# Laying score minima, column terms and inverse sums out block by block, so that each is added in one wide pass

## The reference

```python
# layer 0: 8-head attention, log(clip(adj)) added to the logits, output projection, layer norm of x + out
logits = einsum('bhqd,bhkd->bhqk', q, k) / sqrt(DK) + log(clip(adj, 1e-8, None))[:, None]
out = einsum('bhqk,bhkd->bhqd', softmax(logits), v) @ Wo.T + bo
# layer 1: one head, logits q_i + k_j, masked, leaky, softmax, times feat_proj, + feats
# layer 2: 8-head attention with a bias a_i + c_j + log(adj + 1e-9) on the logits, + x
scores = scores + (a[:, :, None] + c[:, None, :] + b_g + log(adj + EPS))[:, None]
out = einsum('bhij,bjhd->bihd', softmax(scores), V) + x
# layer 3: as layer 1, with other weights
```

## Time and profile before

| What | Value |
|---|---|
| Runs | 1846.76 us median of 3 (1843.98 to 1847.98) |
| Profiled execution | 1851.17 us, span 1849.3 us |
| Mean granted TensorE clock | 0.984 of full |
| Matmuls in the trace | 28388, some 443 for each group |

### The profile page before, as it was taken

One profiled execution on the slowest core, in us unless ns is written; L12 is line 12 of the kernel. 1 busy time (PEld: TensorE's weight loads), 2 busy tenths in 40 slices (PEclk: granted clock), 3 DMA queues, 4 the chain that ended last, 5 costly groups with the idle time before them and its releaser, 6 DMA issues.

```text
span 1849.3 us, 68980 instructions
## 1 busy us (share of the span) xinstructions
PE 1777.7 (96%) x28388; PEld 1679.8 (91%) x28388; DVE 1597.8 (86%) x3486; ACT 1318.2 (71%) x3536; POOL 670.2 (36%) x731
## 2 busy tenths in 40 slices
PE   5899999999999999999999999999999999999985
PEld 5799999999999999999999999999999999999985
DVE  4589889889889889889889889889889889888884
ACT  3577777777777777777777777777777777777763
POOL 2234344344344244244334334334334334334321
PEclk7899999999999999999999999999999999999997
DMA  3010111111111111011011011011011011011000
GB/s 114 19 37 29 44 48 34 40 48 35 38 48 39 34 48 43 30 48 47 26 48 47 26 48 47 25 48 48 25 48 48 25 48 48 25 48 48 25 22 18
DMA packets 48260, 74.57 MB, mean 40 GB/s; under 512 B 5456, under 2 KB 21968, under 8 KB 47952
## 3 DMA queue, kind: packets, MB, share of 16 engines
q1 hardware_dynamic: 47376, 69.49, 11.9%
q10 hardware_dynamic: 576, 0.68, 0.1%
HBM read 53.37 MB, written 16.78 MB: 38 GB/s over the span
## 4 chain that ended last, share of the span: by engine, by line
PE 71%; DVE 21%; issue 6%; ACT 1%; DMA 0%; POOL 0%; DVEq 0%; SPq 0%; POOLq 0%; ACTq 0%
PE banks L870 12%; PE banks L923 12%; PE banks L871 9%; PE banks L872 9%; PE banks L967 7%; PE banks L1062 6%; PE banks L958 6%; DVE xt_lo L650 6%; DVE weights_B L779 5%; DVE logits L723 3%; PE banks L973 3%; DVE logits L719 2%; PE banks L1056 2%; PE banks L1050 2%; PE banks L1022 2%
## 5 line engine op out<-in xcount | busy, mean ns | idle before, releaser
L431 POOL TENSOR_TENSOR xb_t<-sum_t,cols_tile 128x512 f32<-128x512 f32 x128 | 133.2, 1041 | 307.8 <-DVE sum_t L741 301.2
L478 POOL TENSOR_TENSOR weights_A<-weights_A,adj 128x512 f32<-128x512 f32 x64 | 82.5, 1289 | 407.4 <-ACT weights_A L548 407.4
L456 POOL TENSOR_TENSOR xt_lo<-x_t,xt_hi 128x512 fp32r<-128x512 f32 x64 | 82.4, 1288 | 317.1 <-ACT xt_hi L581 317.1
L630 ACT ACTIVATE logits<-logits,f_inv 128x128 f32<-128x128 f32 x256 | 89.0, 395 | 151.2 <-DVE f_inv L840 151.2
L755 DVE TENSOR_REDUCE least_cols_A<-banks 128x4 f32<-128x512 f32 x256 | 169.7, 685 | 15.3 <-PE banks L923 15.2
L779 DVE TENSOR_TENSOR weights_A<-banks,adj 128x512 f32<-128x512 f32 x192 | 132.4, 692 | 52.6 <-ACT banks L548 49.1
L870 PE MATMUL banks<-w_hi_v,xt_hi 128*128 128x258 f32 (+1 forms) x512 | 154.3, 301 | 13.0 <-DVE w_lo_v L650 9.8
L870 PE MATMUL banks<-w_hi_f,xt_hi 128*128 128x258 f32 x512 | 164.0, 320 | 0.8 <-DVE xt_lo L650 0.8
L755 DVE TENSOR_REDUCE least_B<-banks 128x4 f32<-128x512 f32 x256 | 163.9, 682 | 0.9 <-PE banks L932 0.9
L623 ACT ACTIVATE logits<-logits,f_neg_max 128x128 f32<-128x128 f32 x256 | 102.2, 411 | 85.7 <-DVE f_neg_max L726 85.7
L650 DVE TENSOR_TENSOR xt_lo<-sum_t,xt_hi 128x512 fp32r<-128x512 f32 x128 | 154.0, 1203 | 9.3 <-ACT xt_hi L581 2.1
(11 more groups left out here) (181 smaller groups left out, 6210.1 us busy)
## 6 DMA issues: line engine op xcount, KB each, us to landing
x_t<-x_t_dram SPq DMA_DIRECT2D x64, 256.0 KB, 3.6
x_in<-x_dram SPq DMA_DIRECT2D x64, 256.0 KB, 3.8
out_dram<-x_out SPq DMA_DIRECT2D x64, 256.0 KB, 2.4
adj_t<-adj_t_dram SPq DMA_DIRECT2D x64, 128.0 KB, 3.4
adj<-adj_dram SPq DMA_DIRECT2D x64, 128.0 KB, 2.0
scratch<-weights_dram SPq DMA_DIRECT2D x9, 256.0 KB, 7.0
...
```

The source lines that it names most:

```text
L431: return pool.tensor_tensor(result, x, col_tile.unsqueeze(2).broadcast_to([P, KT, GROUP * P]), ALU.add)
```

## The change

Three results that were written as one row for each unit now are written as four blocks of 128 columns, one for each unit, in which all rows but the unit's own are zero. A matmul with all rows of the row group and 512 columns then does for four units what a matmul for each did before.

- Minima and column term: VectorE in place of ScalarE reads the transposed bank, and multiplies it with a mask of 0 and 1 (`pick`) while it writes 128 x 512 elements. `shift` has 4 matmuls in place of 16, `column_terms` 4 in place of 8, all with 32 rows and 512 columns; `minus_pick` is gone, and the weights are `minus`, all -1.
- Inverse sums: VectorE writes both parts as before, now to `inv_both`; GpSimd multiplies them with a mask `own` to `inv_parts`, 128 x 512 (a new step `den` on GpSimd), and `wide` is one matmul of 512 columns with a `spread` of 128 x 128 that sums up the four former ones.
- `ORDER` is new on every engine, and so are some lags.

```diff
-        (0, "again", "A", 0), (0, "shift", "A", 0), (1, "fc", "1", 0), (1, "fc", "1", 1), (4, "turn_p", "3", 0),
...
+        (3, "again", "B", 0), (3, "shift", "B", 0), (4, "mask", "3", 0), (0, "k", "0", 0), (1, "out_proj", "0", 0),
...
+                    elif name == "den":
+                        if G.no == 0:
+                            pool.wait_ge(setup_dve, dve_step["own", "", ""])
+                        pool.wait_ge(inv_split[where], G.no + 1)
+                        pool.tensor_tensor(inv_parts[where][:, :, :],
+                                           inv_both[where][:, :].unsqueeze(1).broadcast_to([P, UNITS, P]),
+                                           own[:, :].unsqueeze(2).broadcast_to([P, UNITS, P]), ALU.mult
+                                           ).then_inc(inv_placed[where], 1)
...
-                    elif name == "turn_max":
-                        act.wait_ge(filled[b], turn.after(G, *key))
-                        act.activation(least_rows[where][:, :], bank[b][:, 0:P], ACT.Copy).then_inc(rows_ready[where], 1)
...
-                    elif name == "turn_rows":
-                        act.wait_ge(filled[b], turn.after(G, *key))
-                        act.activation(c_rows[:, :], bank[b][:, 0:P], ACT.Copy).then_inc(c_rows_ready, 1)
...
+                    elif name == "turn_max":
+                        dve.wait_ge(filled[b], turn.after(G, *key))
+                        dve.tensor_tensor(least_rows[where][:, :, :],
+                                          bank[b][:, 0:P].unsqueeze(1).broadcast_to([P, UNITS, P]),
+                                          pick[:, :].unsqueeze(2).broadcast_to([P, UNITS, P]), ALU.mult
+                                          ).then_inc(rows_ready[where], 1)
+                    elif name == "turn_rows":
+                        dve.wait_ge(filled[b], turn.after(G, *key))
+                        dve.tensor_tensor(c_rows[:, :, :, :],
+                                          bank[b][:, 0:P].unsqueeze(1).unsqueeze(1).broadcast_to([P, GROUP, 2, P]),
+                                          pick[:, 0:GROUP].unsqueeze(2).unsqueeze(2).broadcast_to([P, GROUP, 2, P]),
+                                          ALU.mult).then_inc(c_rows_ready, 1)
...
             def column_terms():
-                for g in range(GROUP):
-                    for r in range(HALF):
-                        part = row_group(r, GROUP)
-                        last = pe.matmul(bank[SCORE_BANKS[r]][:, cols(g, 2 * P)], minus_pick[part, g, :],
-                                         c_rows[part, :].unsqueeze(1).broadcast_to([GROUP, 2, P]),
-                                         start=False, stop=False, skip_group_check=True)
+                for r in range(HALF):
+                    part = row_group(r)
+                    last = pe.matmul(bank[SCORE_BANKS[r]], minus[part, :],
+                                     c_rows[part, :, :, :].rearrange("p g h m -> p (g h m)"),
+                                     start=False, stop=False, skip_group_check=True)
...
             def shift(s, G):
                 pe.wait_ge(rows_ready[s], G.no + 1)
-                for u in range(UNITS):
-                    for r in range(HALF):
-                        part = row_group(r, UNITS)
-                        last = pe.matmul(bank[SCORE_BANKS[r]][:, cols(u)], minus_pick[part, u, :],
-                                         least_rows[s][part, :], start=False, stop=True, skip_group_check=True)
+                for r in range(HALF):
+                    part = row_group(r)
+                    last = pe.matmul(bank[SCORE_BANKS[r]], minus[part, :],
+                                     least_rows[s][part, :, :].rearrange("p u n -> p (u n)"),
+                                     start=False, stop=True, skip_group_check=True)
...
             def wide(s, to):
-                for u in range(UNITS):
-                    last = pe.matmul(to[:, cols(u)], spread[:, u, :, :].rearrange("p r d -> p (r d)"),
-                                     inv_parts[s][:, :], start=True, stop=True)
-                return last
+                return pe.matmul(to[:, :], spread[:, :, :].rearrange("p r d -> p (r d)"),
+                                 inv_parts[s][:, :, :].rearrange("p u n -> p (u n)"), start=True, stop=True)
```

More of the change, by code:

```diff
@@ L27 @@
     "tensor": [
[7 rows of a table removed]
-    "vector": [
-        (3, "max_parts", "B", 0), (1, "split", "A", 0), (2, "mix", "1", 0), (4, "mask", "3", 0),
-        (1, "out_proj", "0", 0), (2, "turn_x", "2", 0), (3, "weigh", "B", 1), (3, "weigh", "B", 2),
-        (3, "weigh", "B", 3), (1, "out_proj", "0", 1), (0, "max", "A", 0), (4, "inv", "3", 0), (1, "norm", "", 0),
[5 rows of a table removed]
-    "scalar": [
[8 rows of a table removed]
[7 rows of a table added]
+    "vector": [
[4 rows of a table added]
+        (0, "out_proj", "0", 1), (3, "inv", "3", 0), (-1, "max", "A", 0), (-1, "max", "A", 1), (0, "norm", "", 0),
[4 rows of a table added]
+    "scalar": [
[7 rows of a table added]
     "gpsimd": [
-        (2, "bias", "2", 0), (0, "bias", "0", 0), (3, "weigh", "B", 0), (1, "penalty", "", 0), (4, "bias", "3", 0),
-        (1, "rstd", "", 0), (0, "weigh", "A", 0), (-1, "turn_x", "0", 0), (-1, "adj_t", "", 0)],
+        (1, "rstd", "", 0), (3, "den", "B", 0), (-1, "turn_x", "0", 0), (0, "bias", "0", 0), (0, "weigh", "A", 0),
+        (0, "den", "A", 0), (-1, "adj_t", "", 0), (2, "weigh", "B", 0), (-1, "penalty", "", 0), (3, "bias", "3", 0),
+        (1, "bias", "2", 0)],
     "sync": [
-        (-1, "load", "", 0), (4, "store", "", 0)],
+        (5, "store", "", 0), (-1, "load", "", 0)],
 }
@@ L169, in build_kernel @@
         inv_hi = {s: sb(f"inv_hi_{s}", [P, P], F32R) for s in "AB"}
-        inv_parts = {s: sb(f"inv_parts_{s}", [P, P], F32R) for s in "AB"}
+        inv_both = {s: sb(f"inv_both_{s}", [P, P]) for s in "AB"}
+        inv_parts = {s: sb(f"inv_parts_{s}", [P, UNITS, P], F32R) for s in "AB"}
         ot = {s: sb(f"ot_{s}", [P, GROUP, DIM]) for s in "AB"}
@@ L252, in build_kernel @@
         inv_split = {s: sem(f"inv_split_{s}") for s in "AB"}
+        inv_placed = {s: sem(f"inv_placed_{s}") for s in "AB"}
         ot_ready = {s: sem(f"ot_ready_{s}") for s in "AB"}
@@ L281, in build_kernel @@
         DVE_STEPS = ([("minus_gamma", "", ""), ("scale", "q0", ""), ("scale", "q2", ""), ("zero", "", ""), ("pick", "", ""),
-                      ("spread", "", ""), ("minus_pick", "", ""), ("low_row", "", "")]
+                      ("own", "", ""), ("spread_sum", "", ""), ("spread", "", ""), ("low_row", "", "")]
                      + [("lo", n, k) for n, k in PARTS + [("soul", "all")]]
@@ L704, in weave_setup @@
                     low_parts(SECOND)
+                elif (name, where) == ("turn_max", "A"):
+                    dve.wait_ge(setup_dve, dve_step["pick", "", ""])
                 elif (name, where, n) == ("weigh", "A", 1):
@@ L789, in turn @@
                         dve.wait_ge(inv_rounded[where], G.no + 1)
-                        dve.scalar_tensor_tensor(inv_parts[where][:, :], inv_den[where][:, :], low_row[:, :],
+                        dve.scalar_tensor_tensor(inv_both[where][:, :], inv_den[where][:, :], low_row[:, :],
                                                  inv_hi[where][:, :].bitcast(F32), ALU.mult, ALU.subtract
@@ L988, in turn @@
                         held.append((key, G.no))
-                    if G.no == 0 and key == ("shift", "A", 0):
-                        pe.wait_ge(setup_dve, dve_step["minus_pick", "", ""])
                     if name == "scores":
@@ L1008, in other @@
                 if name == "wide":
-                    pe.wait_ge(inv_split[layer], G.no + 1)
+                    pe.wait_ge(inv_placed[layer], G.no + 1)
                     return wide(layer, to)
```

37 lines of the change are left out of this document (22 added, 15 removed), and 40 rows, old and new, of the table ORDER.

## The result

| | Before | After |
|---|---|---|
| Median | 1847.37 us (4 runs, 1843.98 to 1848.74) | 1893.14 us (4 runs, 1889.98 to 1895.99) |
| Ratio | | 1.025, 95% interval 1.0228 to 1.0272 |
| Profiled execution | 1851.17 us | 1889.98 us |
| Mean turn (over 37 or 38 turns) | 27.63 us | 28.33 us |

The change makes the kernel 2.5% slower; 1831 was forecast, and the range ended at 1873. The turn grew by 0.70 us, and 64 times that is 45 us, so the whole difference lies in the turn.

The account below looks back on a forecast made before the run. TensorE was taken to bound the kernel before, VectorE after: 25.2 own + 1.9 held + 0.35 waits = 27.45 us a turn against 27.70, times 64 is -16 us, giving 1835, as median 1831; range 1789 to 1873.

Parts of the forecast that it names:

- what holds VectorE in the new order: VectorE's two-input instructions held behind GpSimd passes: four holds, together 1.9 us of a turn against 1.48 before.
- L737: VectorE at mask 3: GpSimd's `weights_B` starts first by 0.3 to 0.4 us and holds it 0.8 to 0.95.
- `xt_lo_2`: On VectorE, 0.8 us after L737, beside one `penalty` pass: held 0.3 us, where it lost 1.06 before.
- `ac` and its copy: Two small VectorE instructions just behind `least_rows_A`, while GpSimd makes `xt_lo_0`: held 0 to 1.2 us, taken as 0.5.
- `sum`: On VectorE, beside GpSimd's `x_0` of 1.1 us: held 0.2 to 0.6 us, taken as 0.25.
- Waits of VectorE: VectorE finds nearly all operands ready in the new order; 0.35 us of waits remain in a turn.
- VectorE's own time: VectorE without any lock: 24.86 - 1.48 + 1.80 for three masked passes = 25.2 us a turn.
- TensorE's savings: Shifts 0.50 us, column terms 0.09, spreads 0.32: 0.91 us a turn, so TensorE needs 26.4.
- TensorE bounds: Rival, chance 0.18: VectorE's holds and waits under 1.2 us, TensorE sets a turn of 26.8, 1789 us.
- The wait for `inv_placed`: TensorE's `wide` after GpSimd's two `inv_parts` passes: added wait costs nothing, at most 1.3 us if late.
- held more, and slower: Rival, chance 0.22: VectorE's two-input instructions fall behind whole GpSimd passes; turn 28.1 us, +26 us, 1873.
- Its threshold: The slower rival decides once VectorE's holds and waits pass 2.5 us of a turn; the forecast had 2.25.

Follow-up runs that it names:

- the fastest version: Kernel after, with GpSimd's `x_0` behind `den` of A and `adj_t` last, and ScalarE's high part of `sum_t_2` ahead of B's first exponential: 1806.80 us, 0.9777.

## Why the prediction was wrong

The step that failed is the one on **what holds VectorE in the new order**: 1.9 us of a turn, where 2.9 were measured. By its terms:

- L737: "0.8 to 0.95". 1.02. GpSimd was first by 0.12 us and not by 0.3 to 0.4, so the hold was nearly the whole pass. The mechanism and the place were right. The reading of the earlier trace rows that a held instruction ends one normal duration behind the pass is 0.14 off (0.55 for 0.69, 0.29 for 0.43).
- `xt_lo_2`: 0.3. Not held (691 ns): the longer hold of L737 carried it to the end of the first `penalty` pass (1025.89 against 1026.00).
- `ac` and its copy: "0 to 1.2, I take 0.5". 0.27 + 1.05 = 1.3, above the upper bound. The bound took one pass for both; each of the two met a pass of its own, since GpSimd starts `x_0` at the moment at which `xt_lo_0` lets `ac` go. And the prediction took only two-input instructions as held; the copy has one input and was held the longest against its own duration. The Trainium skill, "SBUF — State Buffer", section "Who interferes with whom", says that copies from SBUF to SBUF can run in a mode that takes the shared pair too. The trace agrees that the copy is held (0.17 us free, 1.22 behind `x_0`); the mode itself shows in no row.
- `sum`: 0.25. 0.56. A chain again: held by `x_0`, the copy sends `sum` behind the start of `weights_A`, and not beside `x_0`. The prediction had also taken `x_0` at 1.1 us, from 1.48 less a hold of 0.3; it takes 1.28.

The terms around it:

- Waits of VectorE: 0.35; the idle time is 0.85, of which the listed waits are under 0.1. The rest are gaps too short for that list. Added to the 1.0 of the holds this is 1.5 too little.
- VectorE's own time: 25.2; 24.6. In equal orders the three passes cost 1.6 (23.0 to 24.6, and 23.1 to 24.75), where 1.80 was taken. The other 0.4 lies in the rest: 24.86 - 1.48 = 23.4 was taken from the order before, and the new order with the former arithmetic has 23.0. L784 and L790 take 0.69 and 0.68, as forecast. This error goes the other way, 0.6, and the sum 24.6 + 2.9 + 0.85 gives 28.3 in place of 27.45: 0.9 x 64 = 57 us, which with the base (27.63 a turn and not 27.70, 4 us) is the miss of 62.
- TensorE's savings: 0.91 a turn; 2 x 0.16 for the shifts (0.53 each where 0.44 was forecast), 0.01 for the column terms and some 0.3 for the spreads (0.21 for A's, 0.12 for B's), 0.65. The blocks of four row groups with 512 columns take 0.42 to the next row and not 0.34. It had no part in the result, since TensorE didn't bound. It would account for what parts the fastest version (1807) from the 1789 of "TensorE bounds": 0.26 x 64 = 17 us; that TensorE bounds there is not shown.
- The wait for `inv_placed`: nothing, and the spread isn't in TensorE's list of waits. Right in this order; in the order before it showed as 0.64 us a turn.

Of the rivals, "held more, and slower" is what happened. Its threshold was right (2.5 us of holds and waits; they were 3.75, of which VectorE's smaller own time made 0.6 good), and its worst turn of 28.6 holds 28.3. I halved its excess without a reason, and gave it 0.22 though the forecast stood 0.25 us from its threshold, with a term (`ac`) whose bounds were 1.2 us apart. With that, both signs should have had about the same chance.
